# Wide attention: the order of score, projection, fill and value matmuls within a block step

## The chip, the cores and the metric

The kernel runs on one core of one Trainium2 chip. The metric is the device time of one execution in microseconds, on that core.

## The reference, cut to what matters

The program is a network of four layers, each an attention and a feed-forward part, over 16 blocks of 128 tokens with 128 features. The change touches one part alone, the attention of the second layer (L1), which has 16 heads of width 64, all inside one block of tokens, and which is applied twice with the same weights:

```python
HEADS, DIM_HEAD = 16, 64
def _attn_block(q_src, k_src, v_src, Wq, Wk, Wv, Wo, bo):
    q = _split_heads(q_src @ Wq)
    k = _split_heads(k_src @ Wk)
    v = _split_heads(v_src @ Wv)
    dots = jnp.einsum('bhid,bhjd->bhij', q, k) * SCALE
    attn = jax.nn.softmax(dots, axis=-1)
    out = jnp.einsum('bhij,bhjd->bhid', attn, v)
    return out.transpose(0, 2, 1, 3).reshape(...) @ Wo + bo
out = x1 + _attn_block(x1, x2, x2, Wq, Wk, Wv, Wo, bo)
return _attn_block(out, out, x1, Wq, Wk, Wv, Wo, bo)
# x = x + tanh(g_xattn[1]) * (the above, with x1 = layernorm(x), x2 = the context)
```

Everything is float32.

## The kernel before, in words

The program is a list of stages, one after the other, each with its own semaphores. The stage of the change is `wide_attention`. It handles 32 units `u` in order: 16 blocks in the first application of the attention and the same 16 blocks in the second (`U = 2 * NB`). Each engine has its own hand-written program, and the order of a program is the order of the code; nothing plans it. The engines are tied together by semaphores alone.

What one unit needs, by engine and line:

- TensorE fills: `fill(u, n, out)` (L973) makes a half of the keys (n = 0, 1) or of the queries (n = 2, 3), four matmuls of 128 columns into one PSUM bank. `fill_values(u, j, out)` (L977) makes a half of the values, one matmul of 512 columns. ScalarE evicts them (L1099 keys, L1101 queries, L1146 values) and signals `kq` and `v`.
- TensorE scores: `score(u, half)` (L987) multiplies queries by keys for 8 heads. A head has 64 features, so a matmul uses 64 of the array's 128 rows, and two heads lie in the upper and the lower rows. Half 0 writes banks 0 and 1, half 1 banks 2 and 3.
- VectorE: `maximum(u, half)` reduces the scores to row maxima (L1155) and writes scores minus maximum into SBUF (L1159), which signals `sub`. ScalarE takes the exponential (`exponential`, L1106), VectorE sums it and inverts the sum (`total`, L1166 and L1168), and GpSimd multiplies by the inverse (L1089).
- TensorE turns: `turn(u, half)` (L1002) transposes 8 heads of probabilities, by way of banks 4 and 5. ScalarE keeps them (`keep_turned`, L1110, signal `pt`).
- TensorE value matmuls: `gather(u, half)` (L1019) multiplies probabilities by values. An output has 64 rows, so two heads lie in the left and the right columns of the array. Half 0 writes bank 6, half 1 bank 5; ScalarE keeps them (`keep_gathered`, L1114, signal `ot`).
- TensorE projection: `project(u)` (L1034) accumulates 8 products with Wo into bank 7. VectorE's `finish(u)` reads that bank and adds bias and residual (L1174 in the first application, L1179 in the second, where statistics, L1182 and L1184, follow), and signals `read`.

Each fp32 matmul stands in the trace as two MATMUL records (a transpose as one). So a score half is 16 records, a fill 8, a turn 8, a gather 16, a projection 16, and both value fills together 4.

The units are staggered. In step `u` of TensorE's loop the scores are those of unit u, the projection that of u - 2, the fills those of u + 1, the turns and the value matmuls those of u - 1, and the value fills those of u. Bank 7 is shared by the projection, all four fills and the first value fill. So each of these waits until the one before it has been read out of the bank: the first fill waits for `read` of `finish(u - 2)` (L1049), and the other fills and `fill_values` wait for the eviction just before (`kq`). The second value fill goes to bank 4, behind the eviction of the third transposes (`pt`).

VectorE's loop runs `maximum(u, 0)`, `finish(u - 2)`, `maximum(u, 1)`, `total(u, 0)`, `total(u, 1)`. An engine stops at a wait, and everything behind it in its program stops too.

Of the kernel before, what the change touches and what calls it, by code (L numbers as in the profile page):

```python
# [929 lines left out]
def wide_attention(k, tag, out_t):  # L930
# [4 lines left out]
    nc, bank, psum, sub = k.nc, k.bank, k.psum, 2  # L935
# [15 lines left out]
    U = 2 * NB  # L951
# [13 lines left out]
    with nc.Block() as block:  # L965
        @block.tensor
        def _(pe):
            def fill(u, n, out):

                w, src = (wk, k_src(u)) if n < 2 else (wq, q_src(u))  # L970
                for c in range(4):
                    at = (n % 2) * 512 + c * P
                    mm = pe.matmul(out[:, c * P:(c + 1) * P], w[:, at:at + P], src, start=True, stop=True)  # L973
                mm.then_inc(S["fill"], 1)

            def fill_values(u, j, out):
                pe.matmul(out[:, :], v_src(u), wv[:, j * 512:(j + 1) * 512], start=True, stop=True)\  # L977
                  .then_inc(S["fillv"], 1)

            def score(u, half):  # L980
                if u:
                    pe.wait_ge(S["sub"], 2 * u - 1 + half)
                pe.wait_ge(S["kq"], 4 * u + 4)
                for c in range(4):
                    for r in range(2):
                        rows, at = slice(64 * r, 64 * r + 64), half * 512 + c * P
                        mm = pe.matmul(bank[2 * half + r][:, c * P:(c + 1) * P], qt[rows, u % 2, at:at + P],  # L987
                                       kt[rows, u % 2, at:at + P], start=True, stop=True)
                mm.then_inc(S["score"], 1)

            def turn(u, half):
                pe.wait_ge(S["norm"], 2 * u + half + 1)
                for t in (2 * half, 2 * half + 1):
                    if t == 0:
                        pe.wait_ge(S["v"], 2 * u + 2)
                    elif t == 1 and u:
                        pe.wait_ge(S["ot"], 2 * u)
                    elif t > 1:
                        pe.wait_ge(S["pt"], 4 * u + t - 1)
                    for n in range(4):  # L1000
                        c, r = 2 * t + n // 2, n % 2
                        mm = pe.transpose(bank[4 + t % 2][:, n * P:(n + 1) * P],  # L1002
                                          prob[:, u % 2, 8 * half + 4 * r + c % 4, :], k.ident[:, :])
                    mm.then_inc(S["turn"], 1)

            def gather(u, half):
                out = bank[6 - half]
                pe.wait_ge(S["pt"], 4 * u + 2 * half + 2)
                if half == 0:
                    pe.wait_ge(S["v"], 2 * u + 2)  # L1010
                    if u:
                        pe.wait_ge(S["ot"], 2 * u - 1)
                else:
                    pe.wait_ge(S["pt"], 4 * u + 4)
                for c in range(4):
                    t, n = 2 * half + c // 2, 2 * (c % 2)
                    for r in range(2):
                        h = 2 * (4 * half + c) + r
                        mm = pe.matmul(out[64 * r:64 * r + 64, c * P:(c + 1) * P],  # L1019
                                       v[:, u % 2, h * 64:(h + 1) * 64],  # L1020
                                       probt[:, t, (n + r) * P:(n + r + 1) * P], start=True, stop=True)
                mm.then_inc(S["pv"], 1)

            def project(u):
                pe.wait_ge(S["ot"], 2 * u + 2)
                if u + 1 < U:
                    pe.wait_ge(S["v"], 2 * u + 3)
                else:
                    pe.wait_ge(S["read"], u)
                for c in range(8):  # L1030
                    one, other = wo[:, c * P:(c + 1) * P], ot[:, u % 2, c * P:(c + 1) * P]
                    if u >= NB:
                        one, other = other, one
                    mm = pe.matmul(bank[7][:, 0:P], one, other, start=(c == 0), stop=(c == 7))  # L1034
                mm.then_inc(S["out"], 1)

            for n in range(4):
                fill(0, n, bank[4 + n])
            for u in range(U + 2):
                ahead = u + 1 < U  # L1040
                if u < U:
                    score(u, 0)
                if u >= 2:
                    project(u - 2)
                if u < U:
                    score(u, 1)
                if ahead:
                    if u >= 2:
                        pe.wait_ge(S["read"], u - 1)  # L1049
                    elif u == 1:  # L1050
                        pe.wait_ge(S["v"], 1)
                    fill(u + 1, 0, bank[7])
                if 1 <= u <= U:
                    turn(u - 1, 0)
                if ahead:
                    pe.wait_ge(S["kq"], 4 * u + 5)
                    fill(u + 1, 1, bank[7])
                if 1 <= u <= U:
                    turn(u - 1, 1)
                if ahead:  # L1060
                    pe.wait_ge(S["kq"], 4 * u + 6)
                    fill(u + 1, 2, bank[7])
                if 1 <= u <= U:
                    gather(u - 1, 0)
                if ahead:
                    pe.wait_ge(S["kq"], 4 * u + 7)
                    fill(u + 1, 3, bank[7])
                if 1 <= u <= U:
                    gather(u - 1, 1)
                if u < U:  # L1070
                    if ahead:
                        pe.wait_ge(S["kq"], 4 * u + 8)
                    else:
                        pe.wait_ge(S["read"], u - 1)
                    fill_values(u, 0, bank[7])
                    if u:
                        pe.wait_ge(S["pt"], 4 * u - 1)
                    fill_values(u, 1, bank[4])

# [14 lines left out]
        def _(act):  # L1094
            def evict(u, n, src):
                act.wait_ge(S["fill"], 4 * u + n + 1)
                at = slice((n % 2) * 512, (n % 2) * 512 + 512)
                if n < 2:
                    act.activation(kt[:, u % 2, at], src[:, :], ACT.Copy).then_inc(S["kq"], 1)  # L1099
                else:  # L1100
                    act.activation(qt[:, u % 2, at], src[:, :], ACT.Copy, scale=0.125).then_inc(S["kq"], 1)  # L1101

            def exponential(u, half):
                act.wait_ge(S["sub"], 2 * u + half + 1)
                p = prob[:, u % 2, 8 * half:8 * half + 8, :]
                act.activation(p, p, ACT.Exp).then_inc(S["exp"], 1)  # L1106
# [12 lines left out]
            for u in range(U + 1):  # L1119
                ahead, behind = u + 1 < U, u >= 1  # L1120
                if u < U:
                    exponential(u, 0)
                if ahead:
                    evict(u + 1, 0, bank[7])
                if behind:
                    keep_turned(u - 1, 0)
                    keep_turned(u - 1, 1)
                if ahead:
                    evict(u + 1, 1, bank[7])
                if behind:  # L1130
                    keep_turned(u - 1, 2)
                    keep_turned(u - 1, 3)
                if ahead:
                    evict(u + 1, 2, bank[7])
                if u < U:
                    exponential(u, 1)
                if behind:
                    keep_gathered(u - 1, 0)
                if ahead:
                    evict(u + 1, 3, bank[7])  # L1140
                if behind:
                    keep_gathered(u - 1, 1)
                if u < U:
                    for j, src in enumerate((bank[7], bank[4])):
                        act.wait_ge(S["fillv"], 2 * u + j + 1)
                        act.activation(v[:, u % 2, j * 512:(j + 1) * 512], src[:, :], ACT.Copy)\  # L1146
                           .then_inc(S["v"], 1)

        @block.vector
        def _(dve):  # L1150
# [36 lines left out]
            for u in range(U + 2):  # L1187
                if u < U:
                    maximum(u, 0)
                if u >= 2:  # L1190
                    finish(u - 2)
                if u < U:
                    maximum(u, 1)
                    total(u, 0)
                    total(u, 1)

# [568 lines left out]
```

## Time and profile before

| | us |
|---|---|
| median of 3 runs | 1403.89 |
| lowest and highest of them | 1402.46, 1403.98 |
| the profiled execution | 1401.69 |
| its span, first to last instruction | 1399.9 |
| TensorE busy, share of the span | 85% |
| `wide_attention`, from its first fill to its last projection | 271.2 to about 733 |

The profiled execution is 1.8 us longer than its span and 2.2 us shorter than the median. A matmul row of the timeline gives the start of a block of matmuls, then how long it lasted to its modelled end. Since a matmul's end overlaps the start of the next, the difference of two starts says how long TensorE took for a block; the durations of adjacent rows add up to more than that.

### The profile page before, as it was taken

Reading aid. Unit: us, or ns where it says so; the run is one execution under the profiler, and the core shown is the slowest. Engines: PE = TensorE matmul, PEld = TensorE weight load, DVE = VectorE, ACT = ScalarE, POOL = GpSimd, SP = SyncE. Lnnn points to the kernel's source line nnn. Section 1 sums busy time; section 2 is a strip of 40 time slices with the busy share of each in tenths; the row PEclk is TensorE's granted clock in tenths of the full one; section 3 lists DMA queues with packets and bytes.
Section 4 is the critical chain, followed back from the end, with each engine's and each line's share of the span. In section 5 each row is a group of like instructions: output and inputs, shape, how many; then the busy total and the mean of one; then the engine's idle time right before and its main releaser. Section 6 shows DMA issues by size and latency. Waiting matters only on the chain. (4 is left out here: it accounts for less than half of the span.)

```text
span 1399.9 us, 23257 instructions
## 1 busy us (share of the span) xinstructions
PE 1189.1 (85%) x9014; PEld 790.1 (56%) x9029; DVE 839.9 (60%) x1720; ACT 666.3 (48%) x1168; POOL 217.7 (16%) x172
## 2 busy tenths in 40 slices
PE   1877499589999999999998699958579972999998
PEld 1676244468888888888874266622246651444443
DVE  6857534555656565656552489946669987444444
ACT  2686233246565656565654366634346651222221
POOL 2000100123232323232320312110032202000000
PEclk8999799689999999999998799969879995999999
DMA  4500000100000000000000000000000000000000
GB/s 153 177 1 1 0 0 0 60 1 1 1 2 1 1 2 2 1 2 1 1 1 0 0 2 2 1 1 1 0 1 2 2 2 0 0 8 0 8 8 7
DMA packets 6518, 16.06 MB, mean 11 GB/s; under 512 B 1312, under 2 KB 3568, under 8 KB 5520
## 3 DMA queue, kind: packets, MB, share of 16 engines
q1 hardware_dynamic: 6416, 14.66, 3.0%
q8 instruction: 70, 1.15, 0.3%
q14 instruction: 32, 0.26, 0.1%
HBM read 13.60 MB, written 1.05 MB: 10 GB/s over the span
## 5 line engine op out<-in xcount | busy, mean ns | idle before, releaser
L1089 POOL TENSOR_TENSOR work<-work 128x1024 f32<-128x1024 f32 x64 | 121.4, 1897 | 328.4 <-DVE work L1168 328.4
L1155 DVE TENSOR_REDUCE work<-psum 128x8 f32<-128x1024 f32 x64 | 77.9, 1217 | 113.2 <-PE psum L987 113.2
L1288 ACT ACTIVATE work<-psum 128x512 f32<-128x512 f32 x100 | 59.3, 597 | 176.7 <-PE psum L1251 149.1
L1166 DVE TENSOR_REDUCE work<-work 128x8 f32<-128x1024 f32 x64 | 77.7, 1215 | 73.6 <-ACT work L1106 73.6
L1106 ACT ACTIVATE work<-work 128x1024 f32<-128x1024 f32 x64 | 67.3, 1052 | 99.3 <-DVE work L1159 99.3
L1319 DVE TENSOR_TENSOR work<-psum,work 128x512 f32<-128x512 f32 x64 | 44.2, 691 | 104.1 <-PE psum L1263 96.1
L876 ACT ACTIVATE work<-psum 128x512 f32<-128x512 f32 x128 | 72.9, 596 | 66.6 <-PE psum L768 65.7
L1263 PE MATMUL psum<-work,w_down 128*128 128x512 f32 x192 | 98.1, 593 | 0.7
L908 DVE TENSOR_REDUCE work<-psum 128x8 f32<-128x1024 f32 x64 | 75.4, 1219 | 31.8 <-PE psum L756 18.8
L1159 DVE TENSOR_TENSOR work<-psum,work 128x1024 f32<-128x1024 f32 x64 | 78.4, 1225 | 6.4
L768 PEld LDWEIGHTS psum<-ident,work 128*128 128x128 f32 x512 | 56.8, 142 | 43.3 <-issue 29.9
L768 PE MATMUL psum<-ident,work 128*128 128x128 f32 x512 | 75.4, 280 | 6.4 <-ACT work L876 6.1
L987 PEld LDWEIGHTS psum<-work 64*128 64x128 f32 x1024 | 62.9, 190 | 28.8 <-issue 24.3
L384 PE MATMUL psum<-ident,work 128*128 128x128 f32 x128 | 34.4, 461 | 51.7 <-DVE work L362 51.7
L987 PE MATMUL psum<-work 64*128 64x128 f32 x1024 | 74.8, 287 | 0.7 <-ACT work L1101 0.7
L915 DVE TENSOR_TENSOR work<-psum,work 128x1024 f32<-128x1024 f32 x64 | 75.1, 1214 | 0.0
L1247 PE MATMUL psum<-xnt,ctx_tok 128*128 128x512 f32 (+1 forms) x128 | 66.2, 598 | 8.7 <-DVE work L1322 4.9
L873 ACT ACTIVATE work<-work 128x1024 f32<-128x1024 f32 x64 | 65.5, 1052 | 15.3 <-DVE work L915 14.3
L1110 ACT ACTIVATE work<-psum 128x512 f32<-128x512 f32 x128 | 69.1, 597 | 2.4 <-PE psum L1002 2.4
L1019 PE MATMUL psum<-work 128*64 128x128 f32 x1024 | 69.6, 279 | 0.0
L1002 PE MATMUL psum<-ident,work 128*128 128x128 f32 x512 | 66.5, 273 | 0.7 <-ACT work L1110 0.7
L1249 PE MATMUL psum<-xnt,big 128*128 128x512 f32 (+1 forms) x128 | 65.4, 592 | 0.0
(300 smaller groups left out, 2436.6 us busy)
## 6 DMA issues: line engine op xcount, KB each, us to landing
x<-in_x SPq DMA_DIRECT2D x1, 1024.0 KB, 4.8
ctx_tok<-in_ctx SPq DMA_DIRECT2D x1, 1024.0 KB, 6.8
ctxt<-in_ctxt SPq DMA_DIRECT2D x1, 1024.0 KB, 10.1
mask<-in_mask SPq DMA_DIRECT2D x1, 1024.0 KB, 6.9
w_down<-in_down SPq DMA_DIRECT2D x1, 1024.0 KB, 7.2
ctx_tok<-in_g SPq DMA_DIRECT2D x1, 1024.0 KB, 5.9
big<-in_u SPq DMA_DIRECT2D x1, 1024.0 KB, 8.0
out<-x SPq DMA_DIRECT2D x4, 256.0 KB, 2.3
```

What stands on the lines that cost most here:

```text
L768: mm = pe.transpose(bank[4 + g % 2][:, i * P:(i + 1) * P], prob[:, b % 2, h * P:(h + 1) * P], k.ident[:, :])
L876: act.activation(probt[:, g, :], bank[4 + g % 2][:, :], ACT.Copy).then_inc(S["pt"], 1)
L908: dve.tensor_reduce(nmax[:, b % 2, 8 * half:8 * half + 8], s, AX.X, ALU.max, negate=True)\
L915: dve.tensor_tensor(prob[:, b % 2, half * 1024:(half + 1) * 1024] .rearrange("p (h c) -> p h c", c=P), s, nmax[:, b % 2, 8 * half:8 * half ...
L987: mm = pe.matmul(bank[2 * half + r][:, c * P:(c + 1) * P], qt[rows, u % 2, at:at + P], kt[rows, u % 2, at:at + P], start=True, stop=True)
L1019: mm = pe.matmul(out[64 * r:64 * r + 64, c * P:(c + 1) * P], v[:, u % 2, h * 64:(h + 1) * 64], probt[:, t, (n + r) * P:(n + r + 1) * P], s ...
L1089: pool.tensor_tensor(prob[:, u % 2, h, :], prob[:, u % 2, h, :], rinv[:, u % 2, h].unsqueeze(2).broadcast_to([P, 8, P]), ALU.mult)\
L1110: act.activation(probt[:, t, :], bank[4 + t % 2][:, :], ACT.Copy).then_inc(S["pt"], 1)
L1155: dve.tensor_reduce(nmax[:, u % 2, h], s, AX.X, ALU.max, negate=True).then_inc(S["max"], 1)
L1159: dve.tensor_tensor(prob[:, u % 2, h, :], s, nmax[:, u % 2, h].unsqueeze(2).broadcast_to([P, 8, P]), ALU.add)\
L1166: dve.tensor_reduce(rsum[:, u % 2, h], prob[:, u % 2, h, :], AX.X, ALU.add).then_inc(S["sum"], 1)
L1263: pe.matmul(bank[6][:, :], tiles[at[1]][4], h3[:, m, :], start=(at[1] == 0), stop=(at[1] == J - 1)).then_inc(S["down"], 1)
```

## The change

In TensorE's loop the second half of the scores is put right behind the first, ahead of the projection. The fourth fill goes to bank 4 in place of bank 7, right behind the third, and waits for the eviction of the third transposes (`pt`, 4u - 1), except in step 0. The two halves of the value matmuls follow each other. The waits of the value fills are moved by one: the first waits for the third fill's eviction, the second for the fourth's. On ScalarE the eviction of the fourth fill (now from bank 4) stands ahead of both `keep_gathered`. On VectorE `maximum(u, 1)` stands ahead of `finish(u - 2)`. No instruction is added or removed.

```diff
@@ TensorE @@
                 if u < U:
                     score(u, 0)
+                    score(u, 1)
                 if u >= 2:
                     project(u - 2)
-                if u < U:
-                    score(u, 1)
                 if ahead:
                     if u >= 2:
                         pe.wait_ge(S["read"], u - 1)
...
                 if ahead:
                     pe.wait_ge(S["kq"], 4 * u + 6)
                     fill(u + 1, 2, bank[7])
+                if ahead:
+                    if u:
+                        pe.wait_ge(S["pt"], 4 * u - 1)
+                    fill(u + 1, 3, bank[4])
                 if 1 <= u <= U:
                     gather(u - 1, 0)
-                if ahead:
-                    pe.wait_ge(S["kq"], 4 * u + 7)
-                    fill(u + 1, 3, bank[7])
-                if 1 <= u <= U:
                     gather(u - 1, 1)
                 if u < U:
                     if ahead:
-                        pe.wait_ge(S["kq"], 4 * u + 8)
+                        pe.wait_ge(S["kq"], 4 * u + 7)
                     else:
                         pe.wait_ge(S["read"], u - 1)
                     fill_values(u, 0, bank[7])
-                    if u:
+                    if ahead:
+                        pe.wait_ge(S["kq"], 4 * u + 8)
+                    else:
                         pe.wait_ge(S["pt"], 4 * u - 1)
                     fill_values(u, 1, bank[4])
@@ ScalarE @@
                 if u < U:
                     exponential(u, 1)
+                if ahead:
+                    evict(u + 1, 3, bank[4])
                 if behind:
                     keep_gathered(u - 1, 0)
-                if ahead:
-                    evict(u + 1, 3, bank[7])
-                if behind:
                     keep_gathered(u - 1, 1)
@@ VectorE @@
                 if u < U:
                     maximum(u, 0)
+                    maximum(u, 1)
                 if u >= 2:
                     finish(u - 2)
                 if u < U:
-                    maximum(u, 1)
                     total(u, 0)
                     total(u, 1)
```

## Rows read from the trace of the kernel before

**Rows 1.** The page: TensorE busy, share of the span, instructions.

```profile
PE 1189.1 (85%) x9014; PEld 790.1 (56%) x9029; DVE 839.9 (60%) x1720; ACT 666.3 (48%) x1168; POOL 217.7 (16%) x172
```

**Rows 2.** Windows: us, busy (instructions) by engine, granted clock, DMA share, GB/s.

```profile
449.00:589.00 140.00, 140.00 (x1321) 117.10 (x1322) 80.57 (x99) 86.25 (x140) 37.94 (x20) 1.00 0.01 1
```

**Rows 3.** Timeline of TensorE, one unit: start us, us, what, count.

```profile
559.71 1.16 PE L987 MATMUL psum<-work 64*128 64x128 f32 x16
560.80 2.05 PE L1034 MATMUL psum<-w_wo,big 128*128 128x128 f32 x16
562.78 1.16 PE L987 MATMUL psum<-work 64*128 64x128 f32 x16
563.87 1.16 PE L973 MATMUL psum<-big,w_wk 128*128 128x128 f32 x8
...
565.74 1.14 PE L973 MATMUL psum<-big,w_wk 128*128 128x128 f32 x8
566.72 1.04 PE L1002 MATMUL psum<-ident,work 128*128 128x128 f32 x8
567.59 1.14 PE L973 MATMUL psum<-big,w_wq 128*128 128x128 f32 x8
568.66 1.09 PE L1019 MATMUL psum<-work 128*64 128x128 f32 x16
569.68 1.16 PE L973 MATMUL psum<-big,w_wq 128*128 128x128 f32 x8
570.77 1.09 PE L1019 MATMUL psum<-work 128*64 128x128 f32 x16
571.79 1.98 PE L977 MATMUL psum<-w_wv,xnt 128*128 128x512 f32 x4
573.71 1.16 PE L987 MATMUL psum<-work 64*128 64x128 f32 x16
```

**Rows 4.** Timeline of TensorE at the stage's start and at its end.

```profile
277.58 2.06 PE L987 MATMUL psum<-work 64*128 64x128 f32 x32 [0.69 <-ACT work L1101]
279.56 1.16 PE L973 MATMUL psum<-ctxt,w_wk 128*128 128x128 f32 x8
...
287.07 2.07 PE L973 MATMUL psum<-xnt,w_wq 128*128 128x128 f32 x8 [0.69 <-ACT work L1101]
...
720.30 1.99 PE L1019 MATMUL psum<-work 128*64 128x128 f32 x32
722.23 1.98 PE L977 MATMUL psum<-w_wv,xnt 128*128 128x512 f32 x4
```

**Rows 5.** Timeline of VectorE in the unit that begins at 573.71.

```profile
574.92 1.22 DVE L1155 TENSOR_REDUCE work<-psum 128x8 f32<-128x1024 f32 x1 [3.12 <-PE psum L987]
...
577.39 0.34 DVE L1179 SCALAR_TENSOR_TENSOR x<-psum,gate,x 128x128 f32<-128x128 f32 x1
...
578.19 1.19 DVE L1155 TENSOR_REDUCE work<-psum 128x8 f32<-128x1024 f32 x1
...
580.63 1.21 DVE L1166 TENSOR_REDUCE work<-work 128x8 f32<-128x1024 f32 x1
```

**Rows 6.** Timeline of TensorE, three idle times in a later feed-forward stage.

```profile
983.04 1.13 PE L1247 MATMUL psum<-xnt,w_ew 128*128 x2 [2.07 <-DVE work L1313]
...
998.80 2.07 PE L1247 MATMUL psum<-xnt,w_ew 128*128 x2 [2.06 <-DVE work L1313]
...
1007.21 1.12 PE L1256 MATMUL psum<-work,w_comb 128*128 128x512 f32 x2 [2.97 <-DVE work L1336]
```

**Rows 7.** Windows behind these three idle times, columns as in rows 2.

```profile
983.00:986.40 3.40, 3.08 (x7) 1.09 (x8) 3.04 (x5) 1.34 (x2) 0.00 (x0) 1.00 0.00 0
...
998.80:1002.20 3.40, 3.40 (x5) 1.48 (x6) 1.89 (x4) 0.69 (x1) 0.00 (x0) 0.50 0.00 0
1002.20:1005.60 3.40, 2.03 (x5) 0.40 (x3) 3.04 (x5) 1.38 (x2) 0.00 (x0) 1.00 0.00 0
...
1009.10:1015.00 5.90, 1.11 (x4) 0.71 (x4) 2.83 (x13) 1.55 (x3) 0.00 (x0) 0.50 0.00 0
```

## The prediction

> **What bounds the kernel now.** I read the page first: TensorE is busy for 85% of the span, more than any other engine [rows 1]. Then the windows over `wide_attention`: over 140 us in its middle TensorE is busy for 140.00 us, at a granted clock of 1.00, which is the higher level, 2.4 GHz, while VectorE is busy for 80.57 us and ScalarE for 86.25 [rows 2]. So in this stage nothing is late for TensorE, and whatever shortens its own program shortens the stage. The timeline of TensorE then gives the unit: one begins at 559.71 and the next at 573.71, 14.00 us apart [rows 3]. The other engines have slack: VectorE sat idle for 3.12 us before the first maximum of a unit [rows 5].
>
> **The head of the unit, without waits.** Block times are differences of starts. Now it is 1.09 (scores 0), 1.98 (projection), 1.09 (scores 1), 4.16 us up to the first fill at 563.87, and 1.00 for that fill, to 564.87, where its 8 records at the pace inside a block would take less [rows 3]. In unit 0 both halves of the scores already stand together, and they take 1.98 us (277.58 to 279.56), not 2.18 [rows 4]. So a pair of score blocks that touch is 0.20 us cheaper. A block ahead of a half-array block is dearer too: a fill before value matmuls takes 1.07 us (567.59 to 568.66), a fill before transposes 0.98 (565.74 to 566.72) [rows 3]. That is 0.09, and the projection loses it: 1.89. TensorE is thus ready for the first fill 1.98 + 1.89 = 3.87 us after the unit's start, not 4.16. The first fill, no longer behind scores, would save about 0.10 more. A head without waits saves 0.29 + 0.10 = 0.39 us.
>
> **The tail of the unit.** Now fill 2, value matmuls 0, fill 3, value matmuls 1 take 1.07 + 1.02 + 1.09 + 1.02 = 4.20 us, 567.59 to 571.79 [rows 3]. After the change fill 2 takes 0.98, fill 3 also 0.98 (it gains its entry behind scattered blocks, about 0.10, and keeps the 0.09 ahead of a half-array block), and both value matmul halves together 1.93, as at the stage's end (720.30 to 722.23) [rows 4]: 3.89. The saving is 0.31 us. With the head that makes 0.70 us a unit, or 21 us over 30 units, if TensorE never waits.
>
> **The wait that takes its place.** The first fill writes bank 7, and L1049 makes it wait for `read`, which `finish(u - 2)` signals when it has read the projection out of that bank. Now `finish` stands behind one maximum: it begins 3.68 us after the unit (573.71 to 577.39) and lasts 0.34, so it ends at 4.02, ahead of the fill at 4.16 [rows 3, 5]. That is why no wait shows. After the change it stands behind both maxima. The second one, with its subtraction, takes VectorE 2.44 us (578.19 to 580.63) [rows 5], and its scores are there by then, since the joint block ends early. So `finish` ends at 3.68 + 2.44 + 0.34 = 6.46 us, and the fill starts at about 6.5 (a few hundredths for the signal, my estimate). TensorE was ready at 3.87. It stands still for 2.6 us in each unit, and behind the waiting fill in its queue stand the transposes, all other fills, the value matmuls and the next scores; nothing can go around. ScalarE's evictions wait for those. The first fill then pays its 1.00 again.
>
> **The other moved waits** cost nothing. Fill 3 in bank 4 needs the eviction of the third transposes, which goes on while fill 2 runs: at the old spacing fill 3 would start about 4.7 us after fill 0, the transposes were issued at +2.85 to +3.3 and evicted by about +4.2; if not, the price is under 0.5 us a unit. The second value fill needs fill 3's eviction, which on ScalarE is now ahead of the gathered halves; 1.93 us of value matmuls and the first value fill cover it. The steps whose order changes have no DMA, and SyncE's and GpSimd's queues aren't touched.
>
> **The sum, clock at 2.4 GHz.** The fill starts 6.50 - 4.16 = 2.34 us later in the unit, and the tail gives 0.31 back: +2.03, a unit of 16.0 us. The wait exists for u = 2 to 30, 29 units: +59 us. Unit 1 has only the tail's gain, 0.3. Unit 0 loses two waits for an eviction of bank 7, each 0.69 us by the modelled end (one is in front of the fill at 287.07, the other in front of the value fills) [rows 4], about 1.7 us with the pauses around them. Sum: +57, from the bounds +52 (another 0.17 us a unit found) to +62.
>
> **The clock.** A clock of 1.00 over this stage [rows 2] goes with a TensorE that is never idle. The trace shows what idle times of the new size did elsewhere. In the timeline's measure (from a modelled end) the new one will be about 2.45 us. An idle time of 2.07 us left the clock at 1.00, one of 2.06 us was followed by 0.50 (1.2 GHz) for 3.4 us and then by 1.00, one of 2.97 us was followed by 0.50 [rows 6, 7]. Two of three fell. At half clock a fill and transposes take twice their time, so 3.4 us of it cost up to 1.7, and I take 1.65, since a stretch may begin with the end of the idle time. Bounds: no fall in 29 (0 us) and a fall in each (29 x 1.65 = 48 us). I take two thirds of 29, the share of the rows, since the new idle time lies between the two lengths: 19 x 1.65 = 31 us. The Trainium skill, "TensorE: Matmul & The Clock Gate", section "HAM oscillation — how this bites in real kernels", says that an idle time that recurs in each iteration can put the array back to half clock every time. By that rule the sum would stand at the upper bound, near 1507 us; the row at 983.04 speaks against every time [rows 6, 7].
>
> Together: +57 + 31 = +88 on the profiled execution's 1401.7, 1490 us. The median of the runs shown is 2.2 us above that execution, so the runs of the changed kernel should lie from 1490 to 1492; I give 1490.
>
> **The rivals.**
> (a) The wait is there and the clock stays at 1.00: 1403.9 + 57 = 1461 us. For it: one of the three idle times. Against: the other two, and 29 tries.
> (b) Faster. The joint blocks keep their 0.70 us a unit and the fill doesn't wait, so the time is 1403.9 - 21 - 2 = 1381 us. It needs `finish` to be over when TensorE comes to the first fill, at 3.87 us of the unit, or at most 0.70 us later (4.6), from where the kernel is slower. VectorE would have to do two reductions and two subtractions of 1.2 us each between the scores at 1.2 and 4.3 us of the unit; only overlap that the rows don't show could do that. The Trainium skill, "TensorEngine Tiling (Array Packing)", section "Key Properties", says that a change of tiling mode drains TensorE. That is the same gain: the trace agrees, with 1.98 against 2.18 us for the scores [rows 3, 4], and the rule says nothing against it.
> (c) The clock falls in nearly every unit, and the slower first scores delay VectorE as well: 1403.9 + 57 + 48 = 1509 us.
> (d) The wait is smaller than I have it, as VectorE or the projection overlap in a way I miss, half of it: about 1430 us.
>
> **How the numbers follow.** Forecast (wait and falls in a good part of the units) 0.58, (a) 0.24, (c) 0.09, (d) 0.04, (b) 0.05. The range takes in (a) with its lower bound and the forecast with up to 26 falls: 1456 to 1503. Faster by over 0.2% (2.8 us, about what a measurement of this kernel can tell from no change) 0.05; within 0.2% 0.01; slower 0.94. The forecast's own range is 1475 to 1503.
>
> **What would show it.** In the timeline of TensorE the 16 + 16 score records stand as one block of 32, about 1.98 us, the projection behind it takes 1.89, and the first fill starts about 6.5 us into the unit with an idle time of some 2.4 us, released by L1174 or L1179 of the old numbering. The waits list this as TensorE's largest, 29 times. Value matmuls stand as one block of 32 of 1.93 us. Units last 16.0 us at full clock and up to 17.7 where a stretch at 0.50 follows the idle time; the mean is near 17. I am wrong if the first fill starts before 4.6, if the clock over the stage stays at 1.00 (then (a)), or if another wait (fill 3 for `pt`, the second value fill for `kq`) shows.

## The result, and the profile after

| | before | after |
|---|---|---|
| median | 1403.49 us (4 runs, 1402.46 to 1403.98) | 1488.01 us (4 runs, 1483.47 to 1491.92) |
| ratio to before, 95% interval | | 1.0602 (1.0571 to 1.0633) |
| profiled execution, its span | 1401.69, 1399.9 us | 1491.92, 1490.2 us |

The changed kernel is slower by 84.5 us between medians; 1490 was forecast. The profiled execution of the changed kernel is the slowest of its four, so the two traces differ by a little more, 90.3 us of span.

The timeline of TensorE of the changed kernel, one unit in its middle that no change of clock disturbs, then the start of the next, answers to rows 3:

```profile
530.22 2.06 PE L987 MATMUL psum<-work 64*128 64x128 f32 x32
532.20 2.05 PE L1034 MATMUL psum<-big,w_wo 128*128 128x128 f32 x16
536.75 1.16 PE L973 MATMUL psum<-big,w_wk 128*128 128x128 f32 x8 [2.50 <-DVE big L1174]
537.75 1.04 PE L1002 MATMUL psum<-ident,work 128*128 128x128 f32 x8
...
540.47 2.03 PE L973 MATMUL psum<-big,w_wq 128*128 128x128 f32 x16
542.43 1.97 PE L1019 MATMUL psum<-work 128*64 128x128 f32 x32
544.32 1.98 PE L977 MATMUL psum<-w_wv,ctxt 128*128 128x512 f32 x4
546.24 2.06 PE L987 MATMUL psum<-work 64*128 64x128 f32 x32
```

The joint blocks are there: 32 records of scores in 1.98 us, 16 of fills in 1.96, 32 of value matmuls in 1.89. But the first fill starts 6.53 us into the unit (530.22 to 536.75), not 4.16 as in rows 3, and the profile names the releaser, `finish` on VectorE (L1174). The idle time in the bracket, 2.50 us, is counted from the projection's modelled end. The unit lasts 16.02 us.

The timeline of VectorE of the changed kernel, in the unit that begins at 512.76, shows the queue that the fill waits for (rows 5 for before):

```profile
516.44 1.22 DVE L1155 TENSOR_REDUCE work<-psum 128x8 f32<-128x1024 f32 x1
...
518.90 0.34 DVE L1174 SCALAR_TENSOR_TENSOR big<-psum,cols,xnt 128x128 f32<-128x128 f32 x1
```

`finish` begins 6.14 us after the unit, behind the second maximum and its subtraction, and ends at 519.24; the fill starts at 519.30. The projection that it reads had ended at 516.80 (514.75 + 2.05, below), 2.1 us before.

The timeline of TensorE gives also the units where the clock fell. Here is the one from 512.76, of 17.46 us (the next begins at 530.22):

```profile
512.76 2.06 PE L987 MATMUL psum<-work 64*128 64x128 f32 x32
514.75 2.05 PE L1034 MATMUL psum<-big,w_wo 128*128 128x128 f32 x16
519.30 2.08 PE L973 MATMUL psum<-ctxt,w_wk 128*128 128x128 f32 x8 [2.50 <-DVE big L1174]
521.17 1.68 PE L1002 MATMUL psum<-ident,work 128*128 128x128 f32 x8
522.68 1.06 PE L973 MATMUL psum<-ctxt,w_wk 128*128 128x128 f32 x8
```

The same fill takes 1.87 us to the next block, not 1.00, and the transposes 1.51, not 0.87: together 1.51 us more. The second fill gives 0.08 of it back. Windows behind each of the 29 idle times (columns as in rows 2; the granted clock is the third number from the end) show how often this happens. Three of them in a row:

```profile
519.60:522.40 2.80, 2.80 (x14) 2.80 (x14) 0.97 (x2) 0.73 (x2) 1.72 (x1) 0.50 0.00 0
537.00:539.90 2.90, 2.90 (x27) 2.85 (x27) 1.02 (x2) 1.68 (x4) 1.76 (x1) 1.00 0.00 0
553.10:555.90 2.80, 2.80 (x16) 2.80 (x15) 0.94 (x2) 1.11 (x2) 1.74 (x1) 0.51 0.01 3
```

TensorE does 14 or 16 records in these windows at half clock and 27 at full clock. Of the 29 windows 21 are below 1.00.

**Where the 90.3 us are.** The first rows are from the timeline of TensorE of the kernel before, the second from the changed kernel's: first fill of the stage, scores of units 2 and 31, last projection.

```profile
271.19 3.75 PE L973 MATMUL psum<-ctxt,w_wk 128*128 128x128 f32 x16 [0.94 <-PEq L319]
...
307.77 1.16 PE L987 MATMUL psum<-work 64*128 64x128 f32 x16
...
713.71 1.16 PE L987 MATMUL psum<-work 64*128 64x128 f32 x16
...
731.04 2.05 PE L1034 MATMUL psum<-w_wo,big 128*128 128x128 f32 x16 [0.69 <-ACT big L1114]
```

```profile
275.63 3.75 PE L973 MATMUL psum<-ctxt,w_wk 128*128 128x128 f32 x16 [0.94 <-PEq L319]
...
306.80 2.06 PE L987 MATMUL psum<-work 64*128 64x128 f32 x32
...
803.18 2.06 PE L987 MATMUL psum<-work 64*128 64x128 f32 x32
...
820.40 2.05 PE L1034 MATMUL psum<-w_wo,big 128*128 128x128 f32 x16 [0.69 <-ACT big L1115]
```

- Units 2 to 30: 405.94 us before, 496.38 after, +90.4. At 16.02 us a unit 464.6 would do, 58.6 more than before; the other 31.8 are the 21 falls of the clock, 1.51 us each in the mean (the units with a fall last 17.3 to 17.6 us).
- Units 0 and 1: 36.58 before, 31.17 after, -5.4. Some 4 us of this is a stretch at half clock in unit 0 that the trace before happens to have (worked out below).
- Unit 31 to the last projection: 17.33 and 17.22, -0.1.
- Ahead of the stage +4.4 and behind it +0.9, in code that the change doesn't touch. Executions of one kernel differ by as much there: when the changed kernel ran again, its stage began at 272.84, not at 275.63.

### The profile page after: what moved, and what is told of

Same layout as the page of the kernel before. It is cut to its first block and busy times, and to the rows that moved or that the text cites. A ratio compares the mean times of both kernels' runs of the same rounds, so it can differ in the third digit from the quotient of the medians.

```text
span 1490.2 us, 23257 instructions
## 1 busy us (share of the span) xinstructions
PE 1210.0 (81%) x9014; PEld 822.0 (55%) x9029; DVE 838.6 (56%) x1720; ACT 667.7 (45%) x1168; POOL 217.7 (15%) x172
## 5 line engine op out<-in xcount | busy, mean ns | idle before, releaser
L1288 ACT ACTIVATE work<-psum 128x512 f32<-128x512 f32 x100 | 59.3, 597 | 177.9 <-PE psum L1251 149.1
L1107 ACT ACTIVATE work<-work 128x1024 f32<-128x1024 f32 x64 | 67.4, 1053 | 98.4 <-DVE work L1159 98.4
L876 ACT ACTIVATE work<-psum 128x512 f32<-128x512 f32 x128 | 72.8, 596 | 66.8 <-PE psum L768 65.9
L1100 ACT ACTIVATE work<-psum 128x512 f32<-128x512 f32 x64 | 38.3, 598 | 115.1 <-PE psum L973 115.1
L1002 PE MATMUL psum<-ident,work 128*128 128x128 f32 x512 | 82.5, 316 | 0.9 <-ACT work L1111 0.9
L768 PE MATMUL psum<-ident,work 128*128 128x128 f32 x512 | 75.7, 281 | 6.4 <-ACT work L876 6.1
L768 PEld LDWEIGHTS psum<-ident,work 128*128 128x128 f32 x512 | 56.9, 142 | 43.3 <-issue 29.9
L973 PE MATMUL psum<-big,w_wk 128*128 128x128 f32 x256 | 45.6, 334 | 40.0 <-DVE x L1179 32.5
L384 PE MATMUL psum<-ident,work 128*128 128x128 f32 x128 | 34.5, 464 | 51.5 <-DVE work L362 51.5
L973 PE MATMUL psum<-ctxt,w_wk 128*128 128x128 f32 x256 | 46.3, 339 | 37.0 <-DVE big L1174 32.5
L1111 ACT ACTIVATE work<-psum 128x512 f32<-128x512 f32 x128 | 71.3, 597 | 11.1 <-PE psum L1002 10.3
L1002 PEld LDWEIGHTS psum<-ident,work 128*128 128x128 f32 x512 | 74.5, 169 | 1.4 <-issue 1.3
L987 PEld LDWEIGHTS psum<-work 64*128 64x128 f32 x1024 | 59.6, 188 | 24.4 <-issue 23.5
```

Of the source, the lines that this page charges most:

```text
L768: mm = pe.transpose(bank[4 + g % 2][:, i * P:(i + 1) * P], prob[:, b % 2, h * P:(h + 1) * P], k.ident[:, :])
L876: act.activation(probt[:, g, :], bank[4 + g % 2][:, :], ACT.Copy).then_inc(S["pt"], 1)
L1002: mm = pe.transpose(bank[4 + t % 2][:, n * P:(n + 1) * P], prob[:, u % 2, 8 * half + 4 * r + c % 4, :], k.ident[:, :])
```

## The experiments

The experiments were run in three groups, and the kernel before was timed again beside each: its medians were 1400.7 (first two groups) and 1402.5 (third). Differences below are from the median of the group. Single executions of the kernel before spread from 1398.3 to 1404.6 us, so differences of 2 or 3 us between medians are read with care.

### VectorE's order put back

```diff
                 if u < U:
                     maximum(u, 0)
-                    maximum(u, 1)
                 if u >= 2:
                     finish(u - 2)
                 if u < U:
+                    maximum(u, 1)
                     total(u, 0)
```

> The changed kernel with VectorE's order put back (finish between the two maxima), TensorE and ScalarE as changed. Theory (the first fill waits for finish behind both maxima): finish can now start when the projection is done, about 4.1 us into the unit, the fill starts at about 4.5, TensorE idles some 0.5 us, a unit is 14.0 us and the clock stays at 1.00; total 1400 to 1406 us. Rival (the joint blocks themselves cost the time, by bank 4 or by the moved evictions): stays above 1450 us.

1396.9 us, ratio 0.9968 (0.9955 to 0.9981). Its timeline of TensorE:

```profile
561.58 1.16 PE L973 MATMUL psum<-big,w_wk 128*128 128x128 f32 x8 [0.45 <-DVE x L1179]
...
575.55 1.16 PE L973 MATMUL psum<-big,w_wk 128*128 128x128 f32 x8 [0.45 <-DVE x L1179]
```

The unit is 13.97 us and the idle time 0.45. Moving two VectorE instructions takes the whole loss away, with every matmul in its new place. The total lies 3 us below what was expected. The expectation had left out units 0 and 1, which took 31.65 us in this trace against 36.58 before. But the joint blocks' gain is spent: `finish` still can't start before the projection is done, and the projection now ends at about 4 us, too late for a fill that could start at 3.87.

### The tail of the unit alone

The kernel before, with the diff's fill 3, value matmuls, value fills and ScalarE's order, and nothing of its scores or VectorE's order.

> The kernel before with the tail of the unit changed alone (fill 3 in bank 4, both value matmul halves together); scores, projection and VectorE as before. Theory: no wait arises, each unit loses 0.31 us, unit 0 some 2 to 4 us, total 1390 to 1393 us. Rival (fill 3's wait for the third eviction or the second value fill's wait costs): 1403 us or more.

1388.9 us, ratio 0.9910 (0.9875 to 0.9946), 11.8 us below before and 1.1 us below the range expected. Its timeline of TensorE:

```profile
572.35 2.03 PE L973 MATMUL psum<-big,w_wq 128*128 128x128 f32 x16
574.31 1.97 PE L1019 MATMUL psum<-work 128*64 128x128 f32 x32
576.21 1.98 PE L977 MATMUL psum<-w_wv,xnt 128*128 128x512 f32 x4
```

Two fills and both value halves take 3.86 us (572.35 to 576.21), with no idle time; it was 4.20 [rows 3]. This half of the change is sound.

### The head alone

The kernel before with the two score halves joined and `finish` behind both maxima, the tail as before.

> The kernel before with the head changed alone (both score halves together, finish behind both maxima); the tail as before. Theory: the first fill starts 2.34 us later in each of 29 units and nothing comes back: a unit of 16.3 us, +68 us, and about 1.5 us for each of some 20 falls of the clock, +30: 1401 + 98, so 1490 to 1505 us, above the changed kernel by 10 us or more. Rival (the tail's change has a part in the loss): below the changed kernel.

1493.3 us, ratio 1.0659 (1.0625 to 1.0693). Timeline of TensorE:

```profile
567.52 2.06 PE L987 MATMUL psum<-work 64*128 64x128 f32 x32
...
574.05 1.16 PE L973 MATMUL psum<-big,w_wk 128*128 128x128 f32 x8 [2.50 <-DVE big L1173]
...
583.88 2.06 PE L987 MATMUL psum<-work 64*128 64x128 f32 x32
```

The unit at full clock is 16.36 us (567.52 to 583.88) and the idle time the same 2.50. The loss is the head's. One part of the expectation failed: this kernel should have been 10 us or more slower than the changed kernel, and it is 6 us slower (92.6 above before, where the changed kernel run again is 86.8). The tail's 0.34 us a unit is missing, 9.9 us in 29 units, but the clock fell in only 16 of them, not in some 20. The last section comes back to this.

### VectorE's late finish alone

The kernel before with VectorE's part of the diff and nothing else.

> The kernel before with one thing changed, VectorE's order (finish behind both maxima); TensorE as before. Theory: the second maximum waits for the second score half, which ends behind the projection, so finish ends at about 7.05 us and the first fill starts at 7.1 instead of 4.16: a unit of 16.9 us, +85 us, and with the clock 1505 to 1530 us. Rival (the wait comes from TensorE's joint score blocks, VectorE's order is harmless): 1399 to 1405 us.

1505.3 us, ratio 1.0740 (1.0695 to 1.0785): the slowest of all. Its timelines of VectorE and of TensorE:

```profile
581.67 1.23 DVE L1155 TENSOR_REDUCE work<-psum 128x8 f32<-128x1024 f32 x1 [0.52 <-PE psum L987]
...
584.14 0.34 DVE L1174 SCALAR_TENSOR_TENSOR big<-psum,cols,xnt 128x128 f32<-128x128 f32 x1
```

```profile
577.38 1.16 PE L987 MATMUL psum<-work 64*128 64x128 f32 x16
...
584.53 2.08 PE L973 MATMUL psum<-big,w_wk 128*128 128x128 f32 x8 [2.91 <-DVE big L1174]
```

The second maximum now waits for scores that stand behind the projection, so `finish` ends still later and the fill starts 7.15 us into the unit. The joint scores are no cause of the wait; with them it is shorter, 2.50 us against 2.91.

### The projection in another bank

```diff
-                    mm = pe.matmul(bank[7][:, 0:P], one, other, ...)
+                    mm = pe.matmul(bank[6][:, 0:P], one, other, ...)
...
                 if ahead:
-                    if u >= 2:
-                        pe.wait_ge(S["read"], u - 1)
-                    elif u == 1:
-                        pe.wait_ge(S["v"], 1)
+                    if u:
+                        pe.wait_ge(S["v"], 2 * u - 1)
                     fill(u + 1, 0, bank[7])
...
                     if u:
                         pe.wait_ge(S["ot"], 2 * u - 1)
+                        pe.wait_ge(S["read"], u)
```

The last wait is in `gather(u, 0)`, the next to write bank 6. `finish` reads bank 6, the projection's own wait for bank 7 goes, and the last unit's value fill waits for `v` in place of `read`. Otherwise the whole change stands in the kernel, the late `finish` included.

> The changed kernel with the projection in bank 6 in place of bank 7, so that the first fill waits only for the eviction of the value fill, and the first value matmul half waits for read. Theory: the wait of 2.5 us is gone, TensorE is never idle, the clock stays at 1.00 and the joint blocks give 0.70 us a unit: 13.3 us a unit, total 1378 to 1383 us. Rival (VectorE's late finish holds up something else too, or two banks of one chain clash): above 1400 us.

1376.7 us, ratio 0.9824 (0.9799 to 0.9848): 24 us below before, and faster than both kernels. Timeline of TensorE:

```profile
568.32 2.06 PE L987 MATMUL psum<-work 64*128 64x128 f32 x32
570.30 2.05 PE L1031 MATMUL psum<-w_wo,big 128*128 128x128 f32 x16
572.19 1.06 PE L973 MATMUL psum<-big,w_wk 128*128 128x128 f32 x8
573.09 1.04 PE L1002 MATMUL psum<-ident,work 128*128 128x128 f32 x8
```

The projection takes 1.89 us and the first fill 0.90, both as the prediction had them for a head without waits. The total is 1.3 us below the range expected.

The same bank for the projection in the kernel before, nothing joined:

> The kernel before with the projection in bank 6 and nothing joined. Theory (the gain of the changed kernel with bank 6 is the joint blocks', since TensorE had no wait here before): within 2 us of the kernel before. Rival (bank 6 itself gives the gain): 1376 to 1382 us.

1403.4 us, ratio 1.0016 (1.0003 to 1.0028). That is 2.6 us above, just outside what was expected; its unit is 14.00 us (first scores at 570.05 and 584.05), so the stage's middle is unchanged. Where the 2.6 us are isn't shown. A difference of that size comes without any edit: the profiled execution of this kernel, 1398.7 us, spent 32.59 us in units 0 and 1, and that of the kernel before, 1401.7 us, spent 36.58, though the edit changes nothing in them. The bank is worth nothing where nobody waits for it.

And bank 6 with the joint blocks and VectorE's order put back:

> The changed kernel with the projection in bank 6 and VectorE's order put back as well (finish between the maxima). Theory (once the first fill doesn't wait for finish, VectorE has slack and its order is free): within 2 us of the kernel with bank 6 and the late finish, so 23 to 25 us below the kernel before. Rival (the second maximum, now behind the projection, makes the exponentials late and TensorE waits for them): more than 3 us above that.

1376.1 us, ratio 0.9810 (0.9788 to 0.9831): within 0.6 us of the kernel above, as expected, and 26.3 below before, where 23 to 25 was expected. Once the fill doesn't wait for `finish`, its place is free.

### The wait filled with work

These kernels compute matmuls into bank 6 that nobody reads, added work; the rest is the changed kernel.

```diff
                 if u >= 2:
                     project(u - 2)
+                if u >= 2 and ahead:
+                    for c in range(11):
+                        pe.matmul(bank[6][:, 0:P], wk[:, 0:P], k_src(u), start=True, stop=True)
```

> The changed kernel with 11 matmuls more behind the projection in units 2 to 30, whose product nobody reads, about 2.45 us at full clock, so that TensorE works where it stood idle. Theory (the loss has two parts, the wait and the half clock that follows it): the unit stays at 16.0 us, the clock is 1.00 throughout, total 1457 to 1463 us. Rival (the clock costs nothing, since the time is set by the wait alone): 1486 to 1492 us. Second rival (added work pushes the unit): above 1492 us.

1457.8 us, 57.1 above before, ratio 1.0391 (1.0362 to 1.0420). Its timeline of TensorE, in the unit that begins at 562.62, and a window over the stage's middle:

```profile
566.50 2.62 PE L1048 MATMUL psum<-big,w_wk 128*128 128x128 f32 x22
569.16 1.16 PE L973 MATMUL psum<-big,w_wk 128*128 128x128 f32 x8
```

```profile
310.00:700.00 390.00, 388.93 (x3744) 342.01 (x3744) 195.66 (x240) 207.12 (x340) 91.78 (x49) 1.00 0.01 1
```

The fill starts 6.54 us into the unit, as without the added matmuls, and the clock stays at 1.00. Adding 319 matmuls made the changed kernel faster. The changed kernel was run again on the same chip:

> The changed kernel once more, so that it stands beside the part-filled kernels on one chip. Theory: 83 to 87 us above the kernel before, 26 to 30 us above the kernels whose wait is filled with work, which were 56 to 57 above it.

1489.3 us, 86.8 above before, ratio 1.0623 (1.0603 to 1.0644). So the half clock costs 86.8 - 57.1 = 29.7 us (31.5 between the two medians themselves), and the wait 57.1. With 4 matmuls in place of 11:

> The changed kernel with 4 matmuls more behind the projection, 0.9 us, so that TensorE idles 1.6 us in a unit instead of 2.5. Theory (the wait fixes the unit, and an idle time of 1.6 us is among those that left the clock alone in the trace before): unit 16.0 us, clock 1.00, 1455 to 1461 us, as with the wait filled. Rival (any idle time of over a microsecond in each unit brings the half clock): 1475 us or more.

1456.6 us, 55.9 above before, ratio 1.0403 (1.0372 to 1.0433). With 2:

> The changed kernel with 2 matmuls more behind the projection, 0.45 us, so that TensorE idles about 2.05 us in a unit. In the trace before, an idle time of 2.07 us left the clock alone and one of 2.06 us did not. Theory (the share of falls follows the length of the idle time): some falls, 5 to 15 of 29, 1464 to 1480 us where the filled kernel has 1458. Rival (no falls at this length): 1456 to 1460 us. Rival (as many as at 2.5 us): 1484 to 1490 us.

1487.1 us, 84.6 above before, ratio 1.0610 (1.0588 to 1.0633): the forecast of a middle case missed, and the rival of as much as at 2.5 us is right. Below are timelines of TensorE, first with 4, then with 2, then two windows behind idle times of the latter. The three added lines of code move `finish` to L1177 and L1182:

```profile
567.45 1.16 PE L973 MATMUL psum<-big,w_wk 128*128 128x128 f32 x8 [1.61 <-DVE x L1182]
```

```profile
567.28 1.30 PE L973 MATMUL psum<-big,w_wk 128*128 128x128 f32 x8 [2.05 <-DVE big L1177]
```

```profile
534.00:536.80 2.80, 2.80 (x16) 2.80 (x15) 0.94 (x2) 1.07 (x2) 1.75 (x1) 0.50 0.00 0
551.60:554.40 2.80, 2.80 (x27) 2.75 (x26) 0.93 (x2) 1.68 (x4) 1.76 (x1) 1.00 0.01 3
```

With an idle time of 1.61 us a window from 310 to 700 us shows a clock of 1.00; with 2.05 us 19 of 29 windows behind idle times are below it.

## Why the prediction was right

**The bound.** TensorE bound the stage. Shown both ways: taking time out of its program where nothing waits took it out of the total (the tail alone, -11.8; with bank 6, -24), and a wait put into it appeared in full.

**The head and the tail.** The gain of 0.70 us a unit from joint blocks was right. With bank 6 the unit is 13.26 us (transposes at 559.83 and 573.09 in that kernel), 0.74 less than before. The Trainium skill, "TensorEngine Tiling (Array Packing)", section "Key Properties", says that a change of tiling mode drains TensorE. The trace agrees, with 0.74 us for four changes of mode fewer, though no run here tells a drain from another cost of the change.

**The wait that takes its place.** Forecast: `finish` ends at 6.46 us and the fill starts at 6.5. Measured: 519.24 - 512.76 = 6.48 and 6.53 to 6.54. The cause is shown by three kernels: VectorE's order back (loss gone), VectorE's order alone (loss larger), another bank (loss gone with the late order kept). The price was forecast at +59 and came as +58.6.

**The clock.** Forecast: 19 falls at 1.65, 31 us. In the trace: 21 at 1.51, 31.8; by the filled wait 29.7. The two errors cancel. The count rested on three idle times of another stage, two of which were read as falls, and on an assumption that the share follows the length. Neither holds well. Behind the idle time of 2.97 us the matmuls at 1007.21 still ran at full pace, 1.12 us for 2 records where the fallen ones at 998.80 took 2.07, and the clock of 0.50 shows only from 1009.1 on [rows 6, 7]. And the runs don't bear out the assumption (last section). That this term came out so near is luck. The Trainium skill, "TensorE: Matmul & The Clock Gate", section "HAM oscillation — how this bites in real kernels", tells of a kernel that waits some 3 to 5 us in every step and is back at half clock every time. The traces agree in kind: a recurring idle time brought the half clock again and again, and 2.05 us was enough, but it did so in 10 to 21 units of 29, not in each. The prediction's fall in each unit at 2.45 us drew more from that section than its case says, and didn't come.

**Units 0 and 1** gave 5.4 us between the two traces, not 2.0, and that is mostly clock. In the trace before, unit 0 had a stretch at half clock, the fill at 287.07 with 2.07 us for 8 records [rows 4]. The changed kernel's timeline has there:

```profile
289.50 2.05 PE L973 MATMUL psum<-xnt,w_wq 128*128 128x128 f32 x16 [0.69 <-ACT work L1100]
291.39 1.08 PE L977 MATMUL psum<-w_wv,ctxt 128*128 128x512 f32 x2
292.78 1.12 PE L977 MATMUL psum<-w_wv,ctxt 128*128 128x512 f32 x2 [0.31 <-ACT work L1102]
```

Both fills run at full pace, and of the two waits a small one is left, for the fourth fill's eviction, as the second value fill has to wait for it. I had that wait at nothing, true of the units in the middle only. Two more traces part order from clock. The first line is of the kernel with bank 6 alone, whose units 0 and 1 are those of the kernel before; the second is of the changed kernel run again:

```profile
287.10 1.16 PE L973 MATMUL psum<-xnt,w_wq 128*128 128x128 f32 x8 [0.69 <-ACT work L1096]
```

```profile
286.18 3.57 PE L973 MATMUL psum<-xnt,w_wq 128*128 128x128 f32 x16 [0.69 <-ACT work L1100]
```

In the old order the two units take 32.59 us without a stretch at half clock and 36.58 with one. In the new order they take 31.17 without and 31.63 with one, which there covers two fills and little more. So the order by itself gives 1.4 us at full clock, a little less than the 2.0 forecast. The other 4 us are the stretch, which the sum had left out; whether a trace has it is chance (of the changed kernel's two traces one has it), and the new order loses far less by it.

**The other moved waits** cost nothing in the middle, as forecast: the unit shows one idle time and no other.

The rivals: (a), the wait without the clock, is what the filled kernels measure, 57 us. (b), 1381 us, is the kernel with bank 6, 24 us below before. Each needed one more edit than the change made. (c), a fall in nearly every unit, and (d), half the wait, did not come: 21 of 29 units fell, and the fill started as late as forecast.

## What to carry to other kernels

Before an instruction is moved down in an engine's program, list who waits for what stands in the moved place: here a 0.34 us read of one bank released the next matmuls of the bound engine, and two 1.2 us instructions were put ahead of it. Joining blocks of one array mode is worth something only if the buffers between them allow it: here the projection had to leave the bank of the fills for the head's gain to show, and the tail's gain needed no such step. And a recurring wait of the bound engine can cost half as much again in clock, though one of 1.61 us cost none here: filling it with work that nobody reads is a way to measure that part by itself.

## What the runs showed that I had not expected

The loss of clock doesn't simply grow with the idle time. With 1.61 us in each unit no stretch of the middle is slow; with 2.05 us 19 of the 29 windows behind idle times are below 1.00, with 2.50 us 21, and with 2.91 us (late `finish` alone, units of 16.98 us) only 10, where two or three neighbouring units fall and four or five are spared:

```profile
548.30:551.10 2.80, 2.80 (x27) 2.75 (x26) 0.97 (x2) 1.63 (x4) 1.71 (x1) 1.00 0.00 0
565.30:568.10 2.80, 2.80 (x14) 2.80 (x14) 0.95 (x2) 0.75 (x2) 1.73 (x1) 0.50 0.01 3
584.80:587.60 2.80, 2.80 (x14) 2.80 (x15) 1.01 (x2) 0.69 (x2) 1.68 (x1) 0.50 0.00 0
```

Within one kernel every idle time is alike to a hundredth of a microsecond, and still some fall and some don't, in a regular order. So the length of a single idle time doesn't decide it.

The head alone comes nearest to a test of what else does. Its idle time is the same 2.50 us as in the changed kernel, in a unit of 16.36 us instead of 16.02. Its first three units with a wait all fall, and from then on every second one. The next two units after those shown above begin at:

```profile
601.65 2.06 PE L987 MATMUL psum<-work 64*128 64x128 f32 x32
...
618.02 2.06 PE L987 MATMUL psum<-work 64*128 64x128 f32 x32
```

That is 17.77 us for the unit from 583.88 and 16.37 for the next; in all 16 of 29 units fall. In the changed kernel, mostly two in three fall: 21 of 29, and 20 when it ran again. With the same idle time the number of falls thus changes with the unit around it. Its length is one difference, the order of the blocks in its tail another, and no run here parts the two.
